# Four bias additions taken off TensorE and mixer turns written out, in an audio-tower kernel on one Trainium2 core

## The reference

```python
h = token_block(x)                                   # three small convolutions, two layernorms, feed-forward, max over 3 tokens
h = h + recurrence(layernorm(h))                     # h_t = a_t*h_{t-1} + b_t; y = (hs @ C.T + x @ D.T + bias_y) / sqrt(128)
h = h + experts0(layernorm(h))                       # top 2 of 8 experts, hidden 256, and a shared expert
qkv = layernorm(h) @ W_qkv + b_qkv                   # 8 heads of 16, causal linear attention with cos/sin weights
h = h + attention(qkv) @ W_out + b_out
# last block, on n = layernorm(h):
logits = conv3(gelu(conv3(n) + rc_b1)) + rc_b2       # top 2 of 10 experts, hidden 512
h = h + layernorm(n + experts1(n) + conv1(silu(conv9(n) + sh_b1)) + sh_b2)
```

## Time and profile before

| | us |
|---|---|
| median of 3 runs | 1997.2 |
| the 3 runs | 1993.96 to 2009.41 |
| the profiled execution, whole | 2004.29 |
| its span in the trace | 2002.5 |
| mean granted PE clock of it | 0.849 |
| PE busy (8904 MATMUL) | 1604.9 (80%) |
| DVE busy | 928.8 (46%) |
| ACT busy | 473.4 (24%) |
| POOL busy | 548.7 (27%) |

### The profile page before, as it was taken

How to read it: one execution, slowest core, us unless ns; L and a number is a source line. 1 busy time by engine, 2 the same in 40 slices (tenths; PEclk the granted TensorE clock), 3 DMA queues, 4 the chain that set the end, 5 groups by cost and what they waited for, 6 DMA issues and landing times.

```text
span 2002.5 us, 29695 instructions
## 1 busy us (share of the span) xinstructions
PE 1604.9 (80%) x8904; PEld 1215.1 (61%) x8905; DVE 928.8 (46%) x3189; ACT 473.4 (24%) x1133; POOL 548.7 (27%) x888
## 2 busy tenths in 40 slices
PE   6758585577888679768999899979999896999910
PEld 3545463355777558536766576647766565999900
DVE  5574666533444454253313332243313004999978
ACT  2323332121121120221131201321121013555500
POOL 1115253330777500031001300050003102665521
PEclk9767685588999876678998899899998998999955
DMA  5004000002766500000010001010000104666553
GB/s 143 16 1 100 7 25 16 21 26 59 231 210 209 181 12 24 9 19 13 5 36 16 25 5 36 4 36 1 5 5 27 69 9 142 179 182 176 151 157 93
DMA packets 127395, 134.14 MB, mean 67 GB/s; under 512 B 21783, under 2 KB 90621, under 8 KB 127058
## 3 DMA queue, kind: packets, MB, share of 16 engines
q1 hardware_dynamic: 114002, 108.33, 18.9%
q0 software_dynamic: 13312, 24.74, 3.7%
HBM read 98.95 MB, written 38.08 MB: 68 GB/s over the span
## 4 chain that ended last, share of the span: by engine, by line
PE 68%; DVE 11%; another core or an unknown queue 6%; issue 5%; ACT 4%; DVEq 3%; DMA 2%; SPq 1%; POOL 0%; ACTq 0%; POOLq 0%
PE psum L1021 18%; PE psum L842 7%; PE psum L851 6%; PE psum L968 4%; PE psum L949 3%; PE psum L1031 2%; PE psum L1003 2%; PE psum L834 2%; PE psum L219 2%; PE psum L693 2%; PE psum L785 2%; PE psum L992 2%; PE psum L918 2%; PE psum L876 1%
## 5 line engine op out<-in xcount | busy, mean ns | idle before, releaser
L1021 PE MATMUL psum<-NT,wreg 128*128 (+2 forms) x1152 | 403.0, 500 | 7.4 <-ACT conv_h L1243 4.5
L1021 PEld LDWEIGHTS psum<-NT,wreg 128*128 128x128 f32 x1152 | 220.7, 198 | 139.3 <-issue 19.2
L1804 POOL TENSOR_TENSOR rstd<-var_eps,pack 128x6 f32<-128x6 f32 x40 | 53.8, 1346 | 829.1 <-DVE var_eps L1318 829.0
L842 PE MATMUL psum<-work 128*128 128x128 f32 x1664 | 226.8, 280 | 28.2 <-DVE work L1615 28.2
L1843 POOL DMA_INDIRECT rows_out<-work,expert_row_kept x208 | 206.4, 992 | 147.0 <-DVE work L1615 129.2
L842 PEld LDWEIGHTS psum<-work 128*128 128x128 f32 x1664 | 211.1, 198 | 35.1 <-issue 20.1
L693 PE MATMUL psum<-pack,work 128*128 128x128 f32 (+1 forms) x336 | 65.4, 360 | 105.3 <-DVE work L1328 66.5
L1175 ACT ACTIVATE work<-psum,work 128x128 f32<-128x128 f32 x416 | 118.8, 369 | 108.1 <-PE psum L842 108.1
L1615 DVE COPY work<-psum 128x128 f32<-128x128 f32 x208 | 58.8, 283 | 157.3 <-PE psum L834 156.0
L1642 DVE TENSOR_SCALAR work<-psum,expert_row_kept 128x128 f32<-128x128 f32 x208 | 72.8, 350 | 112.0 <-remote 58.6
L693 PEld LDWEIGHTS psum<-pack,work 128*128 128x128 f32 (+1 forms) x336 | 54.5, 191 | 115.1 <-issue 57.5
(11 more groups left out here) (229 smaller groups left out, 2612.3 us busy)
## 6 DMA issues: line engine op xcount, KB each, us to landing
work<-w_and_b SPq DMA_DIRECT2D x104, 258.0 KB
work<-in_ew SPq DMA_DIRECT2D x104, 256.0 KB
work<-rows_in SPq DMA_DIRECT2D x208, 65.0 KB
work<-rows_out SPq DMA_DIRECT2D x32, 384.0 KB, 4.7
rows_out<-work,expert_row_kept POOLq DMA_INDIRECT x208
shared_rows<-conv_rows SPq DMA_DIRECT2D x16, 192.0 KB, 1.9
work<-shared_rows SPq DMA_DIRECT2D x8, 384.0 KB, 5.1
work<-in_xT SPq DMA_DIRECT2D x8, 375.0 KB
```

The costliest lines, as they stand in the source:

```text
L842: r_ = mm(v.ps1[:, c * P:(c + 1) * P], v.w1[:, c * P:(c + 1) * P], v.xT, start=True, stop=True)
L1021: r = mm(conv_bank[m % 2][:, 0:c1 - c0], conv1[:, t * 512 + m * P:t * 512 + (m + 1) * P], nt[:, 0, t + c0:t + c1], start=(t == 0), stop=(t ...
```

## The change

1. **Bias rows.** The five biases now come to SBUF once, as fp32 and broadcast to all partitions (`row_bias`, through a small DRAM buffer). `b_v` is added by POOL to the value tiles that ACT has copied out (`add_b_v`; `cx0` waits for it), `b_out` by POOL to H before the attention output is added (`add_b_out`; the step `h4` waits for it), `b_sh2` by POOL to the kept normalised rows N (`add_b_sh2`), and `b_rc2` by DVE in the step that copied the router's scores. `bias_y` stays on PE, but as an fp32 product of 128 rows with `first_row` (a one in row 0, else zeros). The three-row product stays in `experts1` alone.
2. **main2** has 128 rows instead of 64, the lower ones zero.
3. **Mixer turns** are written out instead of looped: six turns, all wait values constants. `scatter1` moves into the next turn, at position 0.28, right behind `rstd1`.

```diff
-    ("compress", P, P), ("main01", P, 64), ("main2", 64, 64), ("expand", 65, P), ...
+    ("compress", P, P), ("main01", P, 64), ("main2", P, 64), ("expand", 65, P), ...
...
-        rows3 = sb("rows3", [3, (BR + E1) * P], BF16)
...
-        def add_bias(acc, name, n, cols=P):
+        row_bias = sb("row_bias", [P, BR * P])
+        first_row = sb("first_row", [P, P])
+
+        def bias_rows(name, cols=P):
             at = BIAS_ROWS.index(name) * P
-            return nc.tensor.matmul(acc, ones3[:, 0:n], rows3[:, at:at + cols], start=False, stop=True)
+            return row_bias[:, at:at + cols]
...
-        ROUTE_STEPS = [(0.72, "dve onehot"), ..., (0.98, "pool scatter0"), (0.99, "pool scatter1")]
+        ROUTE_STEPS = [(0.72, "dve onehot"), ..., (0.98, "pool scatter0")]
+        LATE_STEPS = [(0.28, "pool scatter1")]
...
-            run(order_a, 0)
-            with eng.Fori(1, ITERS) as i:
-                run(order_a + order_b + order_r, i)
-            run(order_b + order_r, ITERS)
+            lag = {"mix_a": 0, "mix_b": 1, "route": 1, "late": 2}
+            for turn in range(ITERS + 2):
+                for _, phase, x in sorted(order_a + order_b + order_r):
+                    i = turn - lag[phase]
+                    if x.split()[0] != engine or not 0 <= i < ITERS:
+                        continue
...
-            "attention": (ITERS, LANES, ["rstd5", "rstd6"]),
+            "attention": (ITERS, LANES, ["rstd5", "b_out", "b_v", "rstd6", "b_sh2"]),
...
-                    r = mm(v.P[0:64, h, 0:HALF_T], w("main2"), v.h1[0:64, c + 2:c + 2 + HALF_T], start=False, stop=True)
+                    r = mm(v.P[0:64, h, 0:HALF_T], w("main2"), v.h1[:, c + 2:c + 2 + HALF_T], start=False, stop=True)
...
-                    r = add_bias(v.TK[0:n, j, :], "bias_y", n)
+                    r = mm(v.TK[0:n, j, :], first_row[:, 0:n], bias_rows("bias_y"), start=False, stop=True)
...
-                    mm(v.ABt[0:n, j, :], v.nT[:, j * P:j * P + n], w("v"), start=True, stop=False)
-                    r = add_bias(v.ABt[0:n, j, :], "b_v", n)
+                    r = mm(v.ABt[0:n, j, :], v.nT[:, j * P:j * P + n], w("v"), start=True, stop=True)
...
+                    if c == 0:
+                        e.wait_ge(pool_done[k], pool.at("attention", "b_v", k, i))
...
-                    mm(v.ABt[0:n, j, :], v.oT[:, j * P:j * P + n], w("out"), start=True, stop=False)
-                    r = add_bias(v.ABt[0:n, j, :], "b_out", n)
+                    r = mm(v.ABt[0:n, j, :], v.oT[:, j * P:j * P + n], w("out"), start=True, stop=True)
...
-                    r = add_bias(acc, "b_rc2", n, E1)
...
-                        r = add_bias(acc, "b_sh2", n_)
...
+                        r = V.tensor_tensor(sb_[0:n, a:b, 0:ne], src[0:n, a:b, 0:ne],
+                                            bias_rows("b_rc2", ne)[0:n].unsqueeze(1).broadcast_to([n, b - a, ne]), ALU.add)
...
+            def add_b_v(k, i):
+                e.wait_ge(act_done[k], act.at("attention", "v", k, i))
+                for a, b, n in HP:
+                    h = lanes[k].V[0:n, a:b, :, 0:DH]
+                    b_v = bias_rows("b_v")[0:n].rearrange("p (h e) -> p h e", e=DH)
+                    r = G.tensor_tensor(h, h, b_v.unsqueeze(1).broadcast_to([n, b - a, HEADS, DH]), ALU.add)
+                r.then_inc(pool_done[k], pool.step("attention", "b_v", k))
...
             def attention(i, first):
                 for k in range(LANES):
                     rstd("attention", 5, k, i)
+                for k in range(LANES):
+                    add_b_out(k, i)
+                for k in range(LANES):
+                    add_b_v(k, i)
                 if not first:
                     scatter(1, i - 1)
                 for k in range(LANES):
                     rstd("attention", 6, k, i)
+                for k in range(LANES):
+                    add_b_sh2(k, i)
```

82 lines of the change are left out of this document (51 added, 31 removed).

## The result

The changed kernel takes 1944.66 us (median of 4 runs, 1942.18 to 1955.7) against 1996.03 for the kernel before beside it: a ratio of 0.9735, interval 0.9699 to 0.9771. That is 51 us less, where I had forecast 76 less; it lies in the range (1895 to 1962), but above the band that I had given to the forecast itself (1895 to 1937), at the lower edge of rival B's second form (1945 to 1965). The profiled execution has a span of 1942.9 us at a mean granted clock of 0.855.

The account below looks back on a forecast made before the run. PE was taken as the bound, with 68% of the chain, and hand-off chains in round 0 and the mixer. Attention 53 plus mixer 23 gave 76 us off the 1997.2 median: 1921, range 1895 to 1962.

Parts of the forecast that it names:

- rival B: Attention gain only partly out: overlap does not return (first form, 1948) or hand-offs replace products (second, 1945 to 1965); chance 0.18.
- the mechanism of y: Mixer step y: without three-row products the clock rises on the way, 16.4 to 10.9 us, 5.5 gained in turns 1 to 3.
- the price of the three-row product: Bias product on PE in v and out: 0.34 us a tile at full clock, 0.49 at half.
- I take nine tenths: Attention rounds 1 to 3 and tail: of 48.4 us removed from PE, 43.6 come out.
- the 3 us for POOL's adds: Attention: charge for POOL's adds, b_v before cx0, 3 us in all, with 0 and 12 as ends.
- I take the loss as moved, not grown: 0: Attention: scatters moved from projections to chunks delay hand-offs no more than before; 0, with -10 and +50 as ends.
- The mixer term: Mixer: 20.4 us from y and norm1T in turns 1 to 3 plus 3 from main2, 23 in all.
- The moved scatter lets the gain out in turns 2 and 3: Mixer: rstd1 now goes ahead of twelve DMAs, so norm1 is not late when y ends earlier, near 190.
- Turn 4: Mixer turn 4: no gain from shorter y, since rstd4 starts only behind 24 scatter DMAs; 0.
- Rival A: Mixer step y: clock stays at half, so the mixer gives 4 us instead of 23: 1940; chance 0.17.
- D: Rival, attention: POOL's adds hold up cx0, kernel slower, 2037 if a lane's add takes 17 us; chance 0.04.
- Written-out turns: ... I take 0, with +4 and -6 as ends: Mixer: branches and register arithmetic go, code must be fetched; net 0, with +4 and -6 us as ends.

Follow-up runs that it names:

- `mix_only`: Changed kernel with the attention biases back on PE as three-row products and POOL's three adds gone: 1891.11 against 1913.71 us, ratio 0.9872.
- `y_three`: Changed kernel with bias_y again a three-row bf16 product in step y: 1840.04 against 1913.71 us for the kernel before, ratio 0.9618.
- `main2_64`: Changed kernel with main2 as a product of 64 rows again: 1822.97 against 1912.62 us for the kernel before, ratio 0.9532.
- `att_scat_first`: Changed kernel with POOL's scatter ahead of the b_out and b_v adds: 1870.6 against 1912.62 us for the kernel before, ratio 0.9772.

## Why the prediction was right, and where it was off

**Direction, range and the mechanism of y** were right, the range only because it reached into rival B: the two kinds of loss that follow were missing from the forecast itself. The mechanism of y holds, and so does the price of the three-row product. In the traces of the chips of 1914 the four groups of steps (each from its first to its last start, summed over the program) shrink by 18.0 (v), 16.1 (out), 17.9 (router) and 9.8 (convolution) us, 61.8 in all; I had 36.2 for the first two, 8.6 and 15.8, 60.6 in all. The router was under-sized and the convolution over-sized. For the router much of it is the clock: my 0.87 was a tile at the full clock, but in rounds 1 to 3 its steps ran at 0.71 to 0.89 with the three-row product (`mix_only`) and run at 1.0 without. On the chip of 1996 the four groups shrink by 64.3 us, so the tiles came out there too. Rival B's first form (tiles keep their distance, v at 0.42) is out, since v stands at 0.23.

**"I take nine tenths" and the 3 us for POOL's adds** were needless on the chips of 1914: PE's waiting grew by 3 us in all, and no wait of PE at `cx0` is put down to POOL. The stage gave 77 us there (from `mix_only`; nearer 67 from the kernel before), not 53. Of the 24 us more, 5 and 3 are these two terms, 1 the tiles, and some 15 lie in other steps. They are no idle time, and the clock of round 0 rose from 0.62 to 0.68 and that of the rest from 0.96 to 0.97; that the clock is their cause is likely, not shown, and where the form of the mixer sets the length of round 0, part of them belongs to `mix_only` and not to the biases.

**"I take the loss as moved, not grown: 0"** is the term that failed on the chip of 1996. Time in which PE was not busy in rounds 1 to 3 went from 53 to 75 us (my bounds for the next profile were 60 for the forecast and 80 for rival B), and 18 of the 22 us lie in the scatters, which hold PE for 12 to 14 us each where they held it for 7 to 10. This is the second form of rival B, which had 16 each. It took 22 of what the tiles gave.

**The mixer term** was 23: 20.4 for y and `norm1T`, 3 for `main2`, 0 in turn 4. On the chips of 1914 the whole is 24.5 us in the time and 27 in the traces, `y_three` gives 20.4 for the first and `main2_64` 4.6 for the second. On the chip of 1996 it was 9. The step that failed there is "The moved scatter lets the gain out in turns 2 and 3": y ended some 6 us earlier in the turn (71.0 us behind the `rstd2` before it in turn 3, where it was 77.4), but the signals that carry this on arrived only after the scatter that had been moved to that very place. From one step y to the next, turn 1 shrank from 89.6 to 81.1 us, but turn 2 went from 90.5 to 90.2 and turn 3 from 74.7 to 77.9. Before the change y ended past the scatter, and the mixer took as long on this chip as on the others (394.8 and 393.9). I had seen such a late hand-off, but charged it to attention alone, as "put down to issue".

**Turn 4** gained nothing, as said: from `rstd2` of turn 3 to the shared expert it is 98.4 us before and 97.1 after, `rstd4` standing behind 24 DMAs.

**Rival A** is out by the clock in step y; **D** by the 0 us of PE at `cx0` that POOL answers for. `att_scat_first` shows that D's place was well chosen and its price real once POOL's queue is in another order. My bounds of -10 and +50 for the scatters' move into the chunks held as well: PE's waiting grew by 3 us on the chips of 1914 and by 22 on the chip of 1996.

**"Written-out turns: ... I take 0, with +4 and -6 as ends"** failed: at equal order of the scatters they cost 15 to 18 us on the chips of 1914 (0.9562 and 0.9574 against 0.9481). It did not show in my sum because the split, which I had priced only as letting y's gain out, gave as much back (0.9562 to 0.9484, 9 to 14 us of it in the mixer). That these two cancel is luck.

**What stays open** is why signals come late under POOL's indirect DMAs on one chip and not on the others. That they do is read from the traces: waits that end behind the last DMA in the mixer, in the kernel before too in attention, and gaps within the last half of a scatter. Their number alone does not do it: `experts0` and `experts1` hold 104 indirect DMAs each, and `experts0` takes 180 to 189 us there and 153 on the others, while `experts1` takes 228 on both. What differs is how close they stand: POOL issues one every 1.27 us in a scatter and every 1.5 us in `experts0`, but only every 2.2 us in `experts1`. With the late onset of the gaps this looks like something that fills up, which is not shown. No experiment ran under that condition. One candidate is outside the kernel: the Trainium skill (NOTIFIC — the notification-queue block, Interfaces) says that the queue of trace and event records can hold up an engine when an internal buffer fills. No run here shows whether it did.

## What to carry to other kernels

Between products of 128 rows, a bias or a tail of few rows is dear by its height and not by its work: at 128 columns it costs more than a full-height product that is all zeros but for one row (0.36 against 0.22 us), and it can go with a step that stays at 1.2 GHz. Pad it, or better give it to an engine with time; where the products have few columns, measure first (the router gained nothing by padding). When an add moves to POOL, read POOL's whole queue: the adds cost nothing ahead of 24 DMAs and 48 us behind them. Try the parts of a change one at a time: here the third bought nothing, since the split only gave back what the written-out turns cost. And an edit that frees a chain is only worth what the next hand-off lets through, which may differ from one chip or occasion to the next; time it on more than one.

## What the runs showed of the hardware that I had not expected

- The same program took 1996 us on the first occasion and 1913 to 1916 on three chips later (4%); the edit was worth 2.65% then and 5.2% on one of these. The idle time of PE that only the first occasion shows lay where POOL issued indirect DMAs 1.27 to 1.5 us apart, and none where they stood 2.2 us apart.
- On the chip of 1996, finished work of PE was taken up 6.5 to 9.6 us late by DVE and ACT at once, 2 to 3 us after POOL's last scatter DMA; within such a scatter PE also stood 1 to 2 us between its own products, with no wait shown.
- A three-row bf16 product among 128-row fp32 ones costs 0.36 us at the full clock, a 128-row fp32 product 0.22; products of 375 columns that alternate between 64 and 128 rows stand 0.77 us apart, all with 128 rows 0.63.
- Step y ran at 0.50 to 0.55 of the clock, with PE busy 15.00 of 15 us, as long as every third product had three rows, and at 0.73 to 0.85 with 128.
- The same mixer written out instead of looped cost 15 to 18 us, 5 to 7 of them in round 0 of attention, a later stage.
- A POOL add of 128 x 640 fp32 elements takes 1.43 to 1.54 us, DVE's 0.83.
